# A gated delta layer, a ternary network and a mixture of experts on one core: in the middle heads the six convolution taps of the value's first half together, ahead of the substitution for the diagonal blocks

## The reference, cut to what matters

```python
q, k, v = (conv of 4 taps over time of the projected x, then silu)     # 16 key heads, 2 value heads each
M = where(tri_s, (k*beta) @ k.T * decay, 0)           # per chunk
Tinv = solve_triangular(eye + M, eye, lower=True)
u, w = Tinv @ (v*beta), Tinv @ (k*beta*exp(g))
def step(S, inp):                                     # over the chunks
    v_new = u_i - w_i @ S
    o_i = qg_i @ S + a_i @ v_new
    S = S * exp(gl_i) + kd_i.T @ v_new
    return S, o_i
og = o * silu(z); og = og * rsqrt(mean(og*og) + eps) * norm_w
y = og @ W_out
```

## Time and profile before

| | |
|---|---|
| time, median of 3 runs | 1753.99 us (1747.96 to 1755.6) |
| time of the profiled execution | 1748.35 us |
| its span | 1746.4 us |
| TensorE busy | 1513.7 us, 87% |
| VectorE busy | 1049.9 us, 60% |
| ScalarE busy | 857.5 us, 49% |
| GpSimd busy | 489.3 us, 28% |
| mean granted clock of TensorE | 0.945 |

### The profile page before, as it was taken

One profiled execution on the slowest core, in us unless ns is written; L12 is line 12 of the kernel. 1 busy time (PEld: TensorE's weight loads), 2 busy tenths in 40 slices (PEclk: granted clock), 3 DMA queues, 4 the chain that ended last, 5 costly groups with the idle time before them and its releaser, 6 DMA issues. The chain is left out here.

```text
span 1746.4 us, 35670 instructions
## 1 busy us (share of the span) xinstructions
PE 1513.7 (87%) x13996; PEld 1067.1 (61%) x13996; DVE 1049.9 (60%) x2150; ACT 857.5 (49%) x1726; POOL 489.3 (28%) x538
## 2 busy tenths in 40 slices
PE   3538899998998989899898988989799978888999
PEld 2225667676766767667576766766566653554855
DVE  6688676756667575675757667575632242664244
ACT  3335656556555655656556555655443215665210
POOL 3453223332323223223232323233233334110100
PEclk9668999999999999999999999999899988899899
DMA  5022110201101021011111101110300020001100
GB/s 186 30 58 83 26 29 20 59 14 23 29 20 35 14 59 26 11 29 32 22 38 35 29 8 33 28 22 13 95 13 1 1 68 1 2 1 32 42 0 25
DMA packets 142469, 56.39 MB, mean 32 GB/s; under 512 B 109760, under 2 KB 134976, under 8 KB 142048
## 3 DMA queue, kind: packets, MB, share of 16 engines
q1 hardware_dynamic: 132096, 46.10, 11.7%
q10 hardware_dynamic: 10208, 8.01, 1.4%
HBM read 37.11 MB, written 16.97 MB: 31 GB/s over the span
## 5 line engine op out<-in xcount | busy, mean ns | idle before, releaser
L1120 POOL TENSOR_TENSOR og<-og,sz 128x256 f32<-128x256 f32 x128 | 93.2, 728 | 601.2 <-DVE og L1063 393.2
L519 PE MATMUL banks<-wv,xT 128*128 128x512 f32 x256 | 140.4, 691 | 68.2 <-DVE Yv L910 60.9
L910 DVE SCALAR_TENSOR_TENSOR Yv<-banks,cwall,Yv 128x511 f32<-128x511 f32 (+2 forms) x192 | 132.9, 741 | 55.2 <-ACT Yv L750 55.2
L897 ACT ACTIVATE junk<-og 128x512 f32<-128x512 f32 x64 | 40.3, 630 | 189.1 <-POOL og L1120 188.7
L519 PEld LDWEIGHTS banks<-wv,xT 128*128 128x128 f32 x256 | 53.1, 221 | 129.4 <-issue 128.2
L519 PE MATMUL banks<-wqk,xT 128*128 128x512 f32 x256 | 126.8, 622 | 1.4 <-ACT vn L814 1.2
L728 PE MATMUL banks<-wo,oT 128*128 128x256 f32 x512 | 124.3, 385 | 0.8 <-ACT oT L902 0.8
L655 PE MATMUL banks<-wz,xT 128*128 128x256 f32 x512 | 123.5, 384 | 0.0
L1049 DVE TENSOR_TENSOR St<-Sd,banks 128x256 f32<-128x256 f32 x64 | 26.8, 419 | 138.0 <-PE banks L706 134.2
L701 PE MATMUL banks<-V,A 128*128 128x128 f32 x512 | 88.2, 296 | 19.7 <-ACT V L877 19.7
L728 PEld LDWEIGHTS banks<-wo,oT 128*128 128x128 f32 x512 | 92.5, 190 | 21.0 <-ACT oT L902 9.6
(11 more groups left out here) (350 smaller groups left out, 3639.2 us busy)
## 6 DMA issues: line engine op xcount, KB each, us to landing
cm_d<-CM SPq DMA_DIRECT2D x32, 256.0 KB, 4.0
wqk<-in_L_attn_W_qkvz SPq DMA_DIRECT2D x8, 512.0 KB, 4.6
wv<-in_L_attn_W_qkvz SPq DMA_DIRECT2D x8, 512.0 KB, 3.7
wz<-in_L_attn_W_qkvz SPq DMA_DIRECT2D x16, 256.0 KB, 2.9
wo<-in_L_attn_W_out SPq DMA_DIRECT2D x16, 256.0 KB, 3.1
blk<-cm_d SPq DMA_DIRECT2D x128, 16.0 KB, 1.8
t_d<-tb SPq DMA_DIRECT2D x16, 128.0 KB, 1.7
Td<-t_d SPq DMA_DIRECT2D x128, 16.0 KB, 1.8
```

The costliest lines, as they stand in the source:

```text
L519: ins = pe.matmul(bank[b][:, :], xT[:, d, b * S + of_batch, :], w[:, d, :], start=(d == 0), stop=(d == KD - 1))
L910: v.scalar_tensor_tensor(y, bank[b][:, 0:T - j], conv_w(k, t)[:, 3 - j:4 - j], y, ALU.mult, ALU.add).then_inc(s["tap"].sem, 1)
L1120: pool.tensor_tensor(og[:, n, :, :], og[:, n, :, :], sz[q % 2][:, b, :].rearrange("p (h d) -> p h d", h=VR), ALU.mult).then_inc(s["osz"].s ...
```

## The change

Three due times of the table `AT` are changed: the taps 1, 2 and 3 of the value's first half are due at 34.0, 34.05 and 34.1 in place of 34.38, 39.76 and 40.45. The first step of the substitution is due at 34.42.

```diff
 AT = {
...
-    "pv0": 24.24, "pv1": 24.42, "pv2": 24.54, "pv3": 26.83, "v0": 30.77, "v1": 34.38, "v2": 39.76, "v3": 40.45, "vs": 40.39, "pw0": 41.25, "pw1": 41.27, "pw2": 41.29, "pw3": 41.31,
+    "pv0": 24.24, "pv1": 24.42, "pv2": 24.54, "pv3": 26.83, "v0": 30.77, "v1": 34.0, "v2": 34.05, "v3": 34.1, "vs": 40.39, "pw0": 41.25, "pw1": 41.27, "pw2": 41.29, "pw3": 41.31,
```

## The result

The changed kernel takes 1760.86 us (median of 9 runs, 1755.63 to 1772.07) against 1751.05 us before (9 runs, 1747.69 to 1755.6): a ratio of 1.0058 with a 95% interval of 1.0038 to 1.0077, so 9.8 us slower. The prediction was 1775 us, 24 us above that median of before; the measured time lies inside its range, near the lower end. The profiled execution of the changed kernel is at 1772.07 us the slowest of its nine, 23.7 us above the profiled one of before (1748.35), where the sum of terms had given 22.7. Had this profile been the whole evidence, the forecast would have looked right. The explanation has to cover both. A "slow stretch" is a time in which the granted clock is 0.50.

A forecast was written before the change was run, and what follows sets the result against it. The prediction took TensorE's queue, 87% busy, as the bound. Terms of 7.3 and 15.4 us summed to 22.7 on 1748.35, giving 1771; adjusted to the runs' median 1776.7, stated as 1775, range 1759 to 1790.

The forecast's parts named there:

- (a): On VectorE, the four taps moved ahead of the substitution hold up what is behind them by 2.62 us.
- (b): TensorE's wait of 3.45 us before `pw` goes; `pw` runs at full clock for 3.67 us.
- (c): ScalarE's queue behind the later `og` and square keeps `AV` at 719.35, taking the whole gain of 3.45 + 1.70 us.
- (d): Four heads with fast `pw` get the later `AV`, 1.71 us each; with 0.05 in ten others, 7.3 us.
- (e): The diagonal blocks' DMA, 2.62 us later, stays hidden from TensorE, with 2.9 us of cover.
- (f): Clock term: slow stretches on TensorE's work behind the gap before `AV` lose 1.4 us in 11 of 14 heads, 15.4 us.
- the sign that the prediction gave for a clock term too high: In the changed profile, the same wait before `AV` with the clock at 1.00 in the work behind it.
- the neutral case: Rival, chance 0.12: slow stretches fall into TensorE's gap or early, hidden; +7 us at most, 1757 to 1761 us.
- the forecast's own case: The main forecast, chance 0.66: slow stretches cost TensorE clock in 11 of 14 heads, 1764 to 1785 us.

The follow-up runs named there:

- silu_first: Changed kernel with the silu of the value's first half and its table load ahead of the square `junk` on ScalarE: 1732.15 us, ratio 0.9904.
- half_dose: Changed kernel with `v3` put back to 40.45, so only the taps with 510 columns stand ahead of the substitution: 1749.1 us, ratio 0.9997.
- og_first: Changed kernel with `St` and `og` of the recurrence's second turn ahead of the substitution on VectorE: 1767.63 us, ratio 1.0092.
- the two ordinary profiles: Profiled executions of the changed kernel in `again` and `again2`, without edit, near the median time: 1758.29 and 1759.81 us.
- again: Changed kernel run again without edit, for a second profile: 1762.56 us, ratio 1.0086; its profiled execution took 1758.29 us.
- silu_taps_first: Changed kernel with the silu and the second half's first taps ahead of the square `junk` on ScalarE: 1752.91 us, ratio 1.0015.
- again2: Changed kernel run once more without edit, for a third profile; its profiled execution took 1759.81 us.
- before_fill: Kernel before with six additional unused multiplications in TensorE's wait ahead of the value's second projection, in 14 heads: 1758.58 us, ratio 1.0043.

## Why the prediction was right or wrong

**(a), (b), (c): right.** The taps hold the substitution up by 2.6 us, `pw` follows the gate's projection at once and takes 3.60 us (forecast 3.67), and the square's chain puts `AV` at its old place: forecast 12.91 us behind the old place of L995, measured 12.90. `silu_first` shows that it is this chain: the table load and the silu taken out of it, and `AV` moves to 7.83, as worked out beforehand. `half_dose` shows its slack of 1.3 us.

**(d): right in mechanism, half in size.** The heads that had been fast lost their lead: the distance without any loss is 75.2 us, against 73.4 in head 3 of before. From head 1 to head 15 the two ordinary profiles take 8.2 and 9.0 us more than the profiled one of before. With the 4.7 and 5.3 us of the late stretches taken off, 3.4 and 3.6 us are left for (c) and (d), where 7.3 were forecast. Heads 1 to 3, where no late stretch falls, cost 1.5 to 1.8 us each, as forecast, and the slow ones 0.1 (forecast 0.05). The rest went at the end: head 14, counted at 1.71 us more, is 0.8 to 1.2 us shorter than the 77.65 us of before, and heads 12 and 13 are 0.5 to 0.6 us shorter. Why these three are long in the kernel before is open.

**(e): right, with too wide a cover.** The changed kernel has no new wait for `Td` but one of 0.4 us in head 1. But in `og_first` and `silu_first` L574 starts 10.4 to 10.9 us behind L995 when it waits, in head 9 of `og_first` 1.4 us behind the end of the DMA on its queue. So the 2.9 us of cover were about 1.5, and the two kernels that moved `AV` by 2.5 and 3.9 us ran out of it.

**(f): this is the step that failed, by its size.** It took 1.4 us lost in 11 of 14 heads, 15.4 us. The loss in a head that has one is about that: 4.7 / 4 = 1.2 and 5.3 / 4 = 1.3 us in the two ordinary executions, 20.5 / 13 = 1.6 in the one at 1772 us. The number of heads was wrong. In the ordinary executions it is 4, and the whole term 4.7 and 5.3 us, since the other 10 heads have their slow stretch ahead of `pw`, where the wait for `V` hides it. There the sign that the prediction gave for a clock term too high is to be seen: the same place of `AV`, and the clock at 1.00 in the work behind it. The prediction named this kind of head and gave it 3 in 14 in the forecast and 0.12 as a rival for all of them; the truth lies between the two, and the median is 1761, the upper edge of the neutral case. Another 2.9 us of the forecast's excess are its base, a median of 1753.99 us from three runs that is 1751.05 from nine.

The execution at 1772 is near the forecast's own case; it came once in the first nine runs, and 3 of the 12 of `again` were above 1770. That its 23.7 us agree with the sum of 22.7 is in part luck: (f) is 20.5 us there where 15.4 were forecast, and (c) and (d) some 3.6 where 7.3 were.

**The rule of the Trainium skill** in (f) (TensorE: Matmul & The Clock Gate, section "HAM oscillation — how this bites in real kernels"), a burst that starts at half clock behind each wait, gave 19.6 us. The execution at 1772 us, with 20.5, is near it; the ordinary ones, with 4.7 and 5.3 us, are further from it than from the row-based 15.4. A wait does not cost the clock every time here: in each ordinary execution 10 of the 14 waits for `V`, 1.7 to 3.1 us long, are followed by work at full clock, while in the first profile waits of 2.8 us are followed by half clock.

**The slow stretches repeat.** What was missed is that where they fall is no matter of chance from head to head. In the kernel before they begin (by the granted clock in windows of 1 us) at 487.98, 563.08 and 638.18 us, in `again` at 486.24, 561.32 and 636.42, in `silu_taps_first` at 496.44, 571.52 and 646.62: 75.1 us apart each time. A kernel whose heads are 75.2 us long therefore keeps the kind of head that it happens to be in, for a while: in `again` the early stretch begins 4.4 us ahead of L995 in head 4 and 0.1 us earlier with each head, 4.8 us in head 8. In head 9, at 4.9 us, it lasts 3.4 us in place of 6.8 and a late one follows, in head 10 as well; from head 11 on it is back at 4.4. `again2` does the same in heads 5 to 12. So the lossy heads of the ordinary executions come in pairs. Whether a kernel with other distances can be brought into the good kind on purpose was not tried, and why the first profile fell into the alternating kind is open.

## What to carry to other kernels

When a wait is removed, follow every queue that passes the moved work to the same meeting point: here ScalarE's queue behind one late output had 1.3 us of slack against the old bound, so half of the change was free, the whole of it cost 10 us, and moving the silu and its table load ahead of that output turned it into 1% faster than before. In this kernel the time is a floor plus what the clock takes, and the second depends on whether a slow stretch falls on work or ahead of a wait; read both from several profiles, since a single one can be the odd execution. Filling waits with unused multiplications did not pay in any of six kernels.

## What was not expected of the hardware

The same kernel ran at 1755.63 to 1772.07 us. Between its profiled executions, 12 to 14 us apart, the difference goes with the number of heads (4 or 13 of 14) in which TensorE works at 1.2 GHz in place of 2.4 GHz behind a wait. `silu_taps_first` brought `AV` 3.6 us sooner and its heads stayed at 75.0 us, because a slow stretch of 6.8 us settled among four short waits. With added multiplications TensorE stood for 1.7 to 6.2 us in all in heads 1 to 15 with no releaser in the trace (up to 2.05 us at once, in `before_fill`), without them for 0.7 us at most; in head 0 nearly every profile has one such stop, of 0.4 to 1.8 us. In `og_first` a DMA's end on its queue was 1.4 us ahead of the start of the matmul that waited for it.
